# A recurrence walked in half steps, single-head maxima, and 16-bit factors in a six-stage decoder kernel

## The reference

```
1 attn:  h = ln(x); (r, i) = W_to h
         step: s = decay * s + 0.1 * (r, i); rotate by omega; clip to [-10, 10]   # 1024 steps in order
         x2 = x + 0.1 * W_from(states); block = x2 + 0.1 * ffn(ln(x2)), gelu, 1024 hidden
2 xattn: 16 heads of 16 over 154 context tokens, softmax, output projection
3 ffn:   ternary weights, 8-bit activations, depthwise convolution of 3 taps, silu
4 attn:  causal, 16 heads of 64
5 xattn: 16 heads of 64 over 154 context tokens, bias, mask, gate
6 ffn:   x = qdq(x); up = qdq(x Wu); gate = qdq(x Wg); sig = u16(sigmoid(gate))
         gate = qdq(gate * sig); o = qdq(gate * up); out = o Wd
```

## Time and profile before

| what | value |
|---|---|
| median of 2 runs | 2084.41 us (2084.4 to 2084.43) |
| the profiled execution | 2083.63 us, its span 2081.8 us |
| busy TensorE / VectorE / ScalarE / GpSimd | 85% / 69% / 50% / 22% of the span |
| chain that ended last, by engine | TensorE 61%, VectorE 24%, ScalarE 9% |
| first scan to last clip of the recurrence | 30.8 to 522.6 us |
| last model block, from its up projections to the end | 1924 to 2081.8 us |

### The profile page before, as it was taken

The page is one execution under the profiler, slowest core; times in us unless marked ns, Lnnn a source line. Parts: engine busy times, 40 slices in busy tenths (PEclk is TensorE's granted clock), DMA queues, the critical chain, the costliest instruction groups (busy, mean ns, idle before and its releaser), DMA issues.

```text
span 2081.8 us, 34894 instructions
## 1 busy us (share of the span) xinstructions
PE 1778.3 (85%) x12889; PEld 1267.9 (61%) x12889; DVE 1429.1 (69%) x4877; ACT 1046.0 (50%) x2606; POOL 451.8 (22%) x493
## 2 busy tenths in 40 slices
PE   3678888888879779999999999999879999989708
PEld 1356666666653455666667766666648989864307
DVE  6787888887235987767675676776536667653795
ACT  6544565454438535555553455555125545533852
POOL 4000000000000323333333333333212332320002
PEclk7768988898979979999999999999999999999859
DMA  5000000000000111000000000000413432400001
GB/s 155 1 1 1 2 1 1 1 1 1 1 1 15 26 22 66 1 2 1 1 1 1 1 1 1 2 1 1 134 42 81 93 90 65 92 1 0 0 0 41
DMA packets 86078, 49.56 MB, mean 24 GB/s; under 512 B 40223, under 2 KB 83669, under 8 KB 85717
## 3 DMA queue, kind: packets, MB, share of 16 engines
q1 hardware_dynamic: 80195, 47.18, 8.8%
q10 hardware_dynamic: 5714, 0.16, 0.2%
HBM read 45.24 MB, written 2.10 MB: 23 GB/s over the span
## 4 chain that ended last, share of the span: by engine, by line
PE 61%; DVE 24%; ACT 9%; issue 3%; POOL 2%; DMA 0%; ACTq 0%; POOLq 0%; DVEq 0%
PE PS L1661 7%; PE PS L1688 6%; DVE sq L742 6%; DVE nx L739 6%; PE PS L1962 6%; PE PS L1675 5%; PE PS L1646 3%; PE PS L1633 3%; PE PS L2375 3%; PE PS L2025 3%; PE PS L1703 2%; PE PS L1981 2%; PE PS L793 2%; PE PS L1990 2%; PE PS L1622 2%
## 5 line engine op out<-in xcount | busy, mean ns | idle before, releaser
L1727 ACT ACTIVATE px<-PS,cnm 128x128 f32<-128x128 f32 (+7 forms) x256 | 189.5, 741 | 261.7 <-DVE cnm L1775 254.7
L1818 POOL TENSOR_SCALAR px<-px,crl 128x128 f32<-128x128 f32 (+7 forms) x128 | 226.3, 1768 | 412.1 <-DVE crl L1790 412.1
L742 DVE TENSOR_SCALAR sq<-nx 128x4 f32<-128x4 f32 x1024 | 176.4, 172 | 35.2 <-DVE nx L739 0.2
L739 DVE TENSOR_TENSOR_SCAN nx<-sq 128x6 f32<-128x6 f32 x1024 | 174.6, 171 | 35.1 <-POOL sq L878 0.9
L1772 DVE TENSOR_REDUCE cm<-PS 128x1 f32<-128x128 f32 (+6 forms) x224 | 154.2, 688 | 55.0 <-PE PS L1661 54.5
L1675 PE MATMUL PS<-ident,px 128*128 128x128 f32 x1152 | 158.8, 278 | 14.3 <-ACT qT L1715 9.6
L1675 PEld LDWEIGHTS PS<-ident,px 128*128 128x128 f32 x1152 | 129.9, 141 | 61.5 <-issue 34.7
L1661 PE MATMUL PS<-kT,qT 64*128 64x512 f32 (+3 forms) x768 | 159.8, 521 | 5.0 <-ACT px L1727 2.6
L1688 PEld LDWEIGHTS PS<-pT,V 128*64 128x64 f32 x2304 | 124.9, 137 | 63.7 <-issue 34.6
L1688 PE MATMUL PS<-pT,V 128*64 128x128 f32 x2304 | 154.9, 279 | 5.9 <-DVE pT L1783 2.3
L2052 ACT ACTIVATE YT<-YT,xnm 128x154 f32<-128x154 f32 x256 | 104.8, 413 | 92.9 <-DVE xnm L2094 92.9
(11 more groups left out here) (340 smaller groups left out, 3910.3 us busy)
## 6 DMA issues: line engine op xcount, KB each, us to landing
xbs<-in_fside_Bx16xSxS SPq DMA_DIRECT2D x8, 1232.0 KB, 6.6
fsrc<-in_fside_Bx16xSxS SPq DMA_DIRECT2D x8, 1232.0 KB, 6.6
xmk<-in_mask_Bx16xSxS_bk SPq DMA_DIRECT2D x8, 308.0 KB, 8.3
fsrc<-in_mask_Bx16xSxS_bk SPq DMA_DIRECT2D x8, 308.0 KB, 8.3
X<-in_x SPq DMA_DIRECT2D x4, 512.0 KB, 6.8
w<-in_L_attn_W_ffn SPq DMA_DIRECT2D x2, 1024.0 KB, 12.8
t<-in_L_ffn_w SPq DMA_DIRECT2D x2, 1024.0 KB, 11.8
out<-xs SPq DMA_DIRECT2D x16, 128.0 KB, 1.7
```

The lines of the kernel that those rows point to most:

```text
L739: e.tensor_tensor_scan(k.nx[:, :], d0, d1, 0.0, ALU.mult, ALU.add).then_inc(sem("rec.scan"), 1)
L742: e.tensor_scalar(o, bass.AP(k.nx, 2, [[6, P], [0, 2], [3, 2]]), 10.0, -10.0, ALU.min, ALU.max).then_inc(sem("rec.clip"), 1)
L1727: e.activation(k.px[n % 2][:, h, 0:width], src, ACT.Exp, scale=-1.0, bias=k.cnm[:, n % 4, h:h + 1], accum_out=k.cl[:, n % 4, h:h + 1]).the ...
L1818: e.tensor_scalar(k.px[n % 2][:, 0, 0:width], k.px[n % 2][:, 0, 0:width], k.crl[:, n % 4, 0:1], None, ALU.mult).then_inc(sem("c.normal0"), 1)
```

## The change

- **Half steps.** `rec` becomes two steps of the list, `scan` and `clip`, and each chain is offered 0.5 after each of them. The distances keep their numbers (gathered in `GAPS`). `nx` gets two halves, used in turn.
- **Single heads.** `n.top` becomes 16 steps for each tile, each the maximum of one head (154 elements), 0.5 apart. The first 12 replace part 0, at distance 23; `n.score` part 1 follows, then after 3 the last four, then `n.peak`.
- **Smaller pieces.** `n.normal` becomes `n.inverse` and, 1 later, `n.normal`; `n.value` hands its ten VectorE instructions and the two of `tern_clip` to single half steps (`first_chunk`).
- **No carry.** In the last step of a block the clip is done twice, first into the next block's place.
- **`Chain.offer`.** An offer of 100 takes followers up to distance 1 along. So the first "t" in `LAST` puts down all of `ternary_begin`.
- **16-bit factors.** `even` is one multiplication that writes int16 (`gq`) and the sigmoid of it; `gate` writes the sigmoid as uint16 (`sixteen`) and multiplies the two into G; `up` and `second` (the former `times` of ScalarE) write int16, `times` multiplies two int16 tensors into G. `up_` of VectorE goes. U is scaled 4 parts ahead, G 2.

```diff
@@ recurrence_order
-        for n in range(C if c < BT else 0):
-            o.add(("rec", c * C + n))
-            net.offer(1)
-            scores.offer(1)
-            sums.offer(1)
-            ends.offer(1)
+        for n in range(2 * C if c < BT else 0):
+            o.add((("scan", "clip")[n % 2], c * C + n // 2))
+            for chain in (net, scores, sums, ends, other):
+                chain.offer(0.5)
         if c < BT:
-            o.add(("carry", c + 1), ("rec_out", c))
+            o.add(("rec_out", c))
@@ Chain.offer
+        close = 1 if passed >= 100 else 0
...
-            if self.left:
+            if self.left > close:
                 return
+            if close:
+                self.left = 0
@@ recurrence_vector
+    def clip(t):
+        c, n = t // C, t % C
+        state = bass.AP(k.nx, t % 2 * 6 + 2, [[12, P], [0, 2], [3, 2]])
+        place = lambda at: bass.AP(k.sq, at, [[4 * W6, P], [W6, 2], [3, 2]])
+        w.wait_ge("rec.scan", t + 1)
+        if n == C - 1 and c < BT - 1:
+            e.tensor_scalar(place((c + 1) % 2 * 2 * W6 + 1), state, 10.0, -10.0, ALU.min, ALU.max).then_inc(sem("rec.carry"), 1)
+        e.tensor_scalar(place(c % 2 * 2 * W6 + 6 * n + 7), state, 10.0, -10.0, ALU.min, ALU.max).then_inc(sem("rec.clip"), 1)
@@ near_scores
-    yield 5, ("n.score", T, 0)
-    yield 23, ("n.top", T, 0)
-    yield 0, ("n.score", T, 1)
-    yield 6, ("n.top", T, 1)
+    yield g["score"], ("n.score", T, 0)
+    for i in range(12):
+        yield 0.5 if i else g["top"], ("n.top", T, i)
+    yield g["score1"], ("n.score", T, 1)
+    for i in range(12, 16):
+        yield 0.5 if i > 12 else g["top3"], ("n.top", T, i)
@@ near_vector
+    def top(T, i):
+        n = at("n.query", T)
+        m, j = (i % 3, i // 3) if i < 12 else (3, i - 12)
+        w.wait_ge("n.peak", n - 1)
+        w.wait_ge("n.score", 2 * n - (i < 12))
+        e.tensor_reduce(k.nnm[:, m, j, 0:1], PS[:, 4 + j, m % 3 * S2:(m % 3 + 1) * S2], AX.X, ALU.max, negate=True).then_inc(sem("n.max"), 1)
@@ swiglu_order
-    ahead = 3
+    ahead, second = LANES, 2
     o.add(("f.acc", 3), ("f.gm", 3), *[("f.up", v) for v in range(ahead)], ("f.step", 3))
+    o.add(*[("f.second", v) for v in range(second)])
     for v in range(PARTS):
+        if v + second < PARTS:
+            o.add(("f.second", v + second))
+        o.add(("f.times", v))
         if v + ahead < PARTS:
             o.add(("f.up", v + ahead))
-        o.add(("f.times", v))
@@ swiglu_vector
+    def sixteen(v):
+        w.wait_ge("f.sigmoid", v + 1)
+        e.tensor_scalar(k.sq16[:, v % 3, :, :], k.sg[:, v % 3, :, :], 65536.0, 65535.0, ALU.mult, ALU.min).then_inc(sem("f.sixteen"), 1)
...
+        e.scalar_tensor_tensor(g, k.sq16[:, v % 3, :, :], 1.0 / 65536.0, k.gq[:, v % 3, :, :], ALU.mult, ALU.mult).then_inc(sem("f.value"), 1)
...
-    def up_(v):
-        w.wait_ge("f.tu", v + 1)
-        e.tensor_scalar(part(k.U, v), part(k.U, v), MAGIC, None, ALU.subtract).then_inc(sem("f.uq"), 1)
...
-        e.scalar_tensor_tensor(g, g, MAGIC, part(k.U, v), ALU.subtract, ALU.mult).then_inc(sem("f.value"), 1)
+        e.tensor_tensor(g, k.gq[:, v % 3, :, :], k.uq(v), ALU.mult).then_inc(sem("f.value"), 1)
@@ swiglu_scalar, even
-        e.activation(g, g, ACT.Identity, scale=s(6), bias=up).then_inc(sem("f.gq"), 1)
-        w.wait_ge("f.gq", 2 * v + 1)
-        e.activation(g, g, ACT.Identity, bias=down).then_inc(sem("f.gq"), 1)
+        e.mul(q, part(k.G, v), s(6)).then_inc(sem("f.gq"), 1)
```

More of the change, by code:

```diff
@@ L588, in recurrence_order @@
     o = k.order
+    steps = lambda first, last: [(kind, j) for j in range(first, last) for kind in ("scan", "clip")]
     for d in range(DC):
@@ L626, in recurrence_order @@
     o.add(("tails",))
-    o.add(*[("rec", j) for j in range(85, 108)])
+    o.add(*steps(85, 108))
     o.add(("tern_scale",))
-    o.add(("rec", 108))
+    o.add(*steps(108, 109))
     o.add(("tern_inverse",))
@@ L634, in recurrence_order @@
     o.add(*[("n.key", m) for m in range(4)])
-    o.add(*[("rec", j) for j in range(109, C)])
-    o.add(("carry", 1), ("rec_out", 0), ("rec_in", 2))
+    o.add(*steps(109, C))
+    o.add(("rec_out", 0), ("rec_in", 2))
     k.near_tiles = [b * BT + t for t in range(BT) for b in range(B)]
@@ L668, in recurrence_order, with first_chunk @@
         chains[name].offer(100)
+    while any(chain.step for chain in chains.values()):
+        for chain in chains.values():
+            chain.offer(100)
+def first_chunk(third, x0):
+    yield 4, ("tern_int",)
+    yield GAPS["value"] - 4, ("n.value", 0)
+    yield 0, ("n.value", 1)
+    for b in range(B):
+        for i in range(5):
+            yield GAPS["piece"] if b + i == 0 else 0.5, ("n.piece", b, i)
+    for n in range(2):
+        yield 0.5, ("tern_clip", n)
+    for n in third:
+        if n not in x0:
+            yield 0, ("flip", n)
+GAPS = dict(value=14, piece=8, f0=8, f0l=7, sum1=3, shift1=11, turn1=13, up0=2, up=4, down0=6, down1=7, sum2=20, sum2l=12, shift2=8, turn2=10, turn2l=5,
+            score=5, score1=0, top=23, top3=3, peak=0, mix=27, spread=8, normal=20, inv=1, back=4, out=4, sum3=16, shift3=8, r3=20)
 class Chain:
@@ L723, in tern_inverse, with tern_clip, scan @@
         e.reciprocal(k.wsc[:, 4:6], k.wsc[:, 2:4]).then_inc(sem("tern.factor"), 1)
[L725 to L730, removed]
+    def tern_clip(n):
+        w.wait_ge("tern.scalar", n + 5)
+        e.tensor_scalar(k.wi[n][:, :], k.wi[n][:, :], 1.0, -1.0, ALU.min, ALU.max).then_inc(sem("tern.clip"), 1)
+    def scan(t):
         c, n = t // C, t % C
@@ L1123, in normal @@
         own = PS[:, 2 + n % 2, :].rearrange("p (h v) -> p h v", v=32)
-        w.wait_ge("n.spread", n)
-        w.wait_ge("n.back", n - 1)
-        e.reciprocal(k.nrl[:, :], own[:, :, 16]).then_inc(sem("n.rl"), 1)
         w.wait_ge("n.rl", n)
@@ L2392, in swiglu_scalar @@
     s = lambda n: k.stp[:, n:n + 1]
-    up, down = k.magic[:, 0:1], k.magic[:, 1:2]
+    up = k.magic[:, 0:1]
     def input_(i):
```

130 lines of the change are left out of this document (65 added, 65 removed).

## The result

The changed kernel takes **2116.5 us** (median of 2 runs, 2115.84 to 2117.16) where the kernel before takes 2084.41: ratio 1.0154, 95% interval 1.013 to 1.0178, **1.5% slower**. The forecast was 2102, the range 2070 to 2126. Sign and mechanism of the loss hold; its size, 32 us instead of 19, does not.

The account below looks back on a forecast made before the run. A block's period was taken as a stretch set by VectorE plus one set by TensorE. Recurrence +21.5, what follows it +6 and 16-bit factors -8.9 gave +18.6 on 2083.6: 2102 us, range 2070 to 2126.

Parts of the forecast that it names:

- stretch B: TensorE's part of a block, first maxima of b=0 to last of b=1: 39.0 us instead of 28.5.
- Stretch A: VectorE's part of a block, last maxima of b=1 to first of b=0: 27.9 us, 5.0 less.
- the two terms of 1.9 + 0.9: TensorE's part of a block: +1.9 for first maxima spread over half steps, +0.9 for `back` moved behind score part 1.
- +1.5 for the moved query: TensorE's part of a block: query of b=1 moved behind `up` 1, +1.5 us, between 0 and 3.
- +5.4 us in each of blocks 3 to 6: Recurrence: period of each of these blocks 66.9 us against 61.5, +21.8 in all.
- The list is the same but for two things: After the recurrence: only back-to-back maxima (+2) and the ternary beginning put down at once (+4) cost, +6 us.
- rival 4: Last model block's factors: the integer operations run at the double rate, -12.8 us, 2089 us; 8%.
- term (a): Last model block: ScalarE's three operations ahead of a gate become two, saving counted once, -1.6 us.
- Rival 5: Recurrence: the move of `down` does nothing, TensorE's gaps take its 5.3 us in; about 2075 us; 8%.
- Rival 3: VectorE alone sets the recurrence, a block takes 56.5 us; about 2039 us; 6%.
- rival 1: Recurrence: TensorE's clock stays up, some 5 us less in five blocks, -26, 2076 us; 15%.
- rival 2: Recurrence: TensorE's clock stays low, 8 us more in each of five blocks, +40, 2142 us; 9%.

Follow-up runs that it names:

- kernel 9: Changed kernel with distances set so TensorE's and GpSimd's lists are those of the kernel before, ternary beginning step by step: 2076.1 us.
- kernel 10: As kernel 9, with 16 unused transposes ahead of the turn of the second norm in blocks 2 to 6: 2066.7 us.
- kernel 3: Changed kernel with the five steps of the ternary beginning taken one for each t again: 2109.1 us.
- kernel 7: Changed kernel with tile 6's last four maxima, peak and turned behind its first twelve maxima again, after the recurrence: 2120.3 us.
- kernel 1: Kernel before with only the 16-bit factors of the last model block: 2075.8 us.
- kernel 2: Changed kernel with down 0 five steps later, behind the score part 1 of tile b=1 again: 2103.3 us.
- kernel 4: Changed kernel with the first twelve maxima of a tile in one go, which moved all behind them 5.5 steps up: 2126.9 us.
- kernel 5: Changed kernel with the third sum, and with it b=1's query, scores and maxima, 7 steps sooner: 2124.7 us.
- kernel 8: Changed kernel with third sum 7 steps sooner, ternary beginning step by step and tile 6's last maxima sooner together: 2114.8 us.

## Why the prediction was right and where it failed

The mechanism held: the new order of TensorE's list makes stretch B longer, and kernel 9 shows that the order costs the whole 41 us. The sum was 14.9 us short of the profile, by the steps below.

**Stretch A**: 27.9 us predicted, 27.8 measured. The half step's gain of 0.13 us is there. By the prediction's use of the Trainium skill ("VectorE: DVE Perf Modes", "The DRAIN you can't avoid") the stretch would have been 28.7. But the same section adds that a next operation that is not held starts earlier, and the trace agrees with that: in kernels 9 and 10 as in the changed one a maximum between two halves starts 0.07 to 0.08 us after the half in front of it, and the half that depends on that one 0.21 us after it where nothing stands between them. So the prediction was wrong to set the skill against its own rows.

**Stretch B**: 39.0 predicted, 40.5 measured. Two rows of TensorE in block 5 of the kernel before, out and the scores of b=1, are needed beside the earlier trace rows:

```profile
341.27 2.08 PE L1039 MATMUL PS<-x0WoT,nyT 128*128 128x256 f32 x4
...
357.15 1.07 PE L983 MATMUL PS<-nkT,nqT 32*128 32x154 f32 x24
```

Term by term, in block 6 against these: out comes 6.05 us behind the first maximum of b=0, before it was 3.14: +2.9 for the two terms of 1.9 + 0.9. Turn comes at 17.3 instead of 14.4, still +2.9. The scores of b=1 begin at 25.8 instead of 19.0, +6.8: **the moved query costs 3.9, not 1.5**. In it are the two `up` ahead of it, the 1.69 us that TensorE waits for XT in front of them, which the query used to fill, and 0.93 for ScalarE's third sum. From there to score part 1 it is 14.0 instead of 8.9, +5.1 instead of the 6.2, since those two `up` are no longer in it. The step that failed is the term "+1.5 for the moved query" by 2.4 us a block, half made good by the next one.

**The other blocks.** Blocks 4 to 6 gained 6.6 to 6.9 for the 5.4 predicted. Block 3 gained 10.1. "+5.4 us in each of blocks 3 to 6" took block 3's start for 61.5, but it was 60.1: VectorE waited only 0.4 us there, with 10.2 us at half clock. After the change it is like its neighbours, and also waits 1.7 us in front of its first maxima. Blocks 1 and 2 (-1.3, -1.9 for -1.0, -1.8) and 7 (+1.9 for +2.5) came as said. The recurrence: +29.2 for +21.5.

**Behind the recurrence**: 12.8 for 6. The turns and scalings ahead of tile 7's scores measured 5.1 (kernel 3) for 4. The other 7.7 lie almost wholly ahead of down 0: that starts 47.2 us after the recurrence in kernel 3 and 39.6 before the change. **"The list is the same but for two things" failed**: at the recurrence's end the chains stood elsewhere. Tile 6's first twelve maxima started 0.9 us behind the last clip and now start 4.9 us behind it, its peak and turned stand behind two `up`, and the mix of tile 13 ran at the half clock (1.78 us instead of 1.08). Kernel 7 mended one of these and gained nothing; kernel 9, with TensorE's list as before, has 94.3. The step that failed is that the list's order was taken as kept. The 2 us for four tiles of maxima did not show: with the order kept and the half steps in (kernel 9) the stretch is 2.8 us shorter than with the factors alone.

**The 16-bit factors**: -9.0 by kernel 1 for -8.9, but -11.0 between the marks in the profile. Groups and a timeline of VectorE in the last model block, for the earlier trace rows:

```profile
L2371 DVE SCALAR_TENSOR_TENSOR G<-sq,gq 128x1536 f32<-128x1536 uint16 x8 | 14.1, 1759 | 0.3
L2379 DVE TENSOR_TENSOR G<-gq,oq 128x1536 f32<-128x1536 int16 x8 | 14.0, 1750 | 1.6 <-ACT gq L2461 1.6
...
L2365 DVE TENSOR_SCALAR sq<-sg 128x1536 uint16<-128x1536 f32 x8 | 7.6, 947 | 0.0
```

```profile
2029.81 0.16 DVE L2324 TENSOR_REDUCE acc<-mx 128x1 f32<-128x8 f32 x1
...
2033.90 1.76 DVE L2379 TENSOR_TENSOR G<-gq,oq 128x1536 f32<-128x1536 int16 x1 [1.64 <-ACT gq L2461]
...
2061.65 0.16 DVE L2324 TENSOR_REDUCE acc<-mx 128x1 f32<-128x8 f32 x1
```

Products of two 16-bit tensors take 1.75 us, as with float, so rival 4 is out, and the trace agrees, for a float result, with the Trainium skill's rule on two-source operations ("VectorE: DVE Perf Modes", "What auto-detection actually checks"). Between the stages it is 4.1 us (predicted 4.1), the eight products take 27.75 (27.6). From the first scale of this model block to that behind the gates it is 3.8 us less for the 1.6 of term (a), as in kernel 1, and 2.3 to 2.4 less in kernels 2, 3 and 9; why it varies is open.

**The rivals.** Rival 5 (the move of `down` does nothing) is refuted by kernel 2 for B, but half of it is true of the sum: moved out of B, down 0 fills A. Rival 3 never came near; its 2039 also leaves out the +6 for the end, with which it is 2044. Rivals 1 and 2 spoke of one clock for all blocks; the time at half clock grew by 3.5 us a block, at the end of A. Kernel 9 shows that rival 1 was the better place to look: with the order right, blocks of the same list differ by 3 us with the clock.

The forecast's own range doesn't follow from its bounds, either: taken end to end they give 2076 to 2117 and not 2085 to 2122. The measured time lies inside the wide range. Of the 14.9 us that were missing, 6.8 lie behind the recurrence, 4.7 in block 3 and 4.2 in blocks 4 to 6.

So what costs is shown: with TensorE's list as before the whole 41 us go. How they divide among the moves isn't, since the single distances moved other entries with them, and kernels 2, 4, 5 and 8 lost 7 to 11 us in block 7 for it.

## What to carry to other kernels

Where two engines hand over to each other twice per round, write down which stretch each sets, and cost a reordering by the entries that it puts *ahead of what the other engine waits for*; then ask whether the other stretch has room for what is taken out. A finer interleaving on one engine and the order on the other are two changes: hold the second one's list fixed while the first is tried; only then does the finer one show its worth. A distance in a list that is counted in steps moves everything behind it, so compare whole lists after each edit, not the edited entries, and look at every block: the gain of kernel 2 in four blocks was 19 us, and block 7 took 7 of them back.

## What the runs showed of the hardware

- Two blocks of the same kernel, 59.4 and 62.4 us long, do the same work; behind the maxima of b=0 the granted clock was 1.00 and 0.52, and from out to the turn it took 6.7 and 10.5 us.
- Work that nothing needs can make a kernel faster: 16 transposes, 1.9 us, in an idle stretch of TensorE gave 9 us between the medians of kernels 9 and 10, whose runs overlap (2068 to 2081 and 2062 to 2072). With whole steps and maxima in blocks, under the same list, they gave nothing (2077.0 against 2075.8).
- The changed kernel and five experiments had periods of 68.2 to 68.3 us in some or all of their blocks, with half-clock times of 17 to 24 in these. One and the same list of TensorE had 17.1 and 20.5 with it (the changed kernel and kernel 7). What ties them to one value is open.
- A maximum of 154 elements between two halves of a recurrence step made the distance 0.30 us instead of 0.21, so that the maximum, 0.31 us by itself, cost the chain 0.09.
